# GRU gates of a recurrent block on one core: r and z share 64-row passes, their sigmoids run in halves, and VectorE copies the turned h

## The reference

```
adj  = relu(x.reshape(b, 1600) @ masker_param[t] + masker_bias[t]), rows normalised   # b, t, 50, 50
m    = adj @ (x @ weight)                                                             # b, t, 50, 32
gates = m @ w_ih.T + b_ih + x @ w_hh.T + b_hh ; r, z, ng = split(gates, 3)
r = sigmoid(r); z = sigmoid(z); ng = tanh(r * ng)
h = (1 - z) * ng + z * x
... batch norm over the 2048 samples, layer norm per sample, attention over the nodes, weighted sum -> (b, 64)
```

## Time and profile before

| | |
|---|---|
| time of three runs, median (lowest to highest) | 2565.87 us (2556.56 to 2578.45) |
| the profiled execution's own time | 2563.58 us |
| its span | 2561.6 us |
| mean granted TensorE clock | 0.965 of full speed |
| TensorE matmul, busy | 2367.9 us, 92% |
| TensorE weight load, busy | 1913.5 us, 75% |
| VectorE, busy | 1049.4 us, 41% |
| ScalarE, busy | 814.4 us, 32% |
| GpSimd, busy | 560.3 us, 22% |

### The profile page before, as it was taken

How to read it: one execution, slowest core, us unless ns; L and a number is a source line. 1 busy time by engine, 2 the same in 40 slices (tenths; PEclk the granted TensorE clock), 3 DMA queues, 4 the chain that set the end, 5 groups by cost and what they waited for, 6 DMA issues and landing times. The chain is left out here.

```text
span 2561.6 us, 34873 instructions
## 1 busy us (share of the span) xinstructions
PE 2367.9 (92%) x12466; PEld 1913.5 (75%) x12466; DVE 1049.4 (41%) x1771; ACT 814.4 (32%) x1353; POOL 560.3 (22%) x365
## 2 busy tenths in 40 slices
PE   6899999999979999999999994999999999975788
PEld 4788888888867888888888873888888888852333
DVE  3432233333224333223333312565656666575446
ACT  2321222222223222122222212444444444535341
POOL 0000000000000000000000000567677676764130
PEclk9999999999999999999999996999999999987889
DMA  5412222221244211222222005454545455318430
GB/s 152 121 67 83 83 83 83 83 80 43 70 133 134 82 51 62 83 83 83 83 83 81 30 28 164 132 166 131 170 134 158 142 154 153 118 63 236 122 88 5
DMA packets 178886, 262.63 MB, mean 103 GB/s; under 512 B 11370, under 2 KB 160558, under 8 KB 175534
## 3 DMA queue, kind: packets, MB, share of 16 engines
q1 hardware_dynamic: 162706, 235.74, 30.6%
q10 hardware_dynamic: 16128, 26.22, 2.9%
HBM read 194.22 MB, written 67.70 MB: 102 GB/s over the span
## 5 line engine op out<-in xcount | busy, mean ns | idle before, releaser
L326 PE MATMUL psum<-w_hi,x_lo 128*128 128x500 f32 x2080 | 826.6, 397 | 32.2 <-DVE x_lo L187 15.6
L326 PE MATMUL psum<-w_lo,x_hi 128*128 128x500 f32 (+1 forms) x2080 | 814.4, 392 | 0.0
L326 PE MATMUL psum<-w_hi,x_hi 128*128 128x500 f32 x1920 | 749.7, 390 | 0.0
L326 PEld LDWEIGHTS psum<-w_hi,x_lo 128*128 128x128 f32 x2080 | 394.1, 189 | 111.2 <-issue 20.6
L267 DVE TENSOR_REDUCE rows<-u 128x10 f32<-128x500 f32 x160 | 107.6, 672 | 895.4 <-ACT u L221 895.0
L326 PEld LDWEIGHTS psum<-w_lo,x_hi 128*128 128x128 f32 (+1 forms) x2080 | 395.1, 190 | 75.7
L326 PEld LDWEIGHTS psum<-w_hi,x_hi 128*128 128x128 f32 x1920 | 363.6, 189 | 74.3
L620 POOL MEMSET share<- 128x1 f32 x1 | 0.1, 98 | 1540.0 <-POOLq L79 1540.0
L227 ACT COPY at<-psum 128x640 f32<-128x640 f32 x160 | 110.7, 692 | 690.6 <-PE psum L308 690.6
L686 PE MATMUL psum<-adj_sb,xs_sb 100*64 100x100 f32 x2048 | 200.6, 350 | 30.5 <-DMA xs_sb<-xz 30.5
L686 PEld LDWEIGHTS psum<-adj_sb,xs_sb 100*64 100x64 f32 x2048 | 145.0, 149 | 73.4 <-issue 63.7
(11 more groups left out here) (169 smaller groups left out, 2832.6 us busy)
## 6 DMA issues: line engine op xcount, KB each, us to landing
w_raw<-W SPq DMA_DIRECT2D x120, 500.0 KB, 6.7
adjT<-at SPq DMA_DIRECT2D x320, 125.0 KB
adj_sb<-adjT SPq DMA_DIRECT2D x16, 2500.0 KB
xs_sb<-xz SPq DMA_DIRECT2D x16, 1600.0 KB
hF<-hC ACTq DMA_DIRECT2D x96, 256.0 KB, 3.5
h<-hF SPq DMA_DIRECT2D x64, 256.0 KB, 4.2
x_raw<-xT SPq DMA_DIRECT2D x16, 832.0 KB
xg_sb<-xg SPq DMA_DIRECT2D x16, 800.0 KB, 19.6
```

Of the source, the lines that this page charges most:

```text
L326: last = nc.tensor.matmul(mm_out(w % 2), a[0:r, k, cols], b[0:r, k, :], start=k == 0 and n == 0, stop=k == KF and n == 1)
```

## The change

- r and z no longer have passes of their own. The weights `wd` hold two sets of 128 columns: `RZ_W`, in which the rows of two sample groups (64 rows) lead to 128 outputs, r and z of both, and `N_W`, block-diagonal as before. For each of the six terms two matmuls are issued, one on rows 0 to 63 into bank 2, one on rows 64 to 127 into bank 3. In bank 2 r of its two groups is in partitions 0 to 63 and z in 64 to 127, in bank 3 the other way round, so that r lies where n of the same group lies, and z is in the other half.
- n comes after the turns now, and `gates_done` after n. The r-z block waits for `r_ready` and `z_ready` of the round before.
- Each sigmoid is two instructions of 64 partitions. z's write to a fourth bank (`z_bank`, bank 4, one for all rounds) in the other partition half and wait for `h_ready` of the round before.
- VectorE makes the copy of the turned chunks (`evacuate`), between `update` and `finish`, and after the last tile all seven batches ahead of its statistics. ScalarE issues the store after z's sigmoids and before the tanh.
- The setup on VectorE copies the weights in 24 pieces instead of 8.

```diff
-        wd = sb("wd", [P, 2, 3, P])
+        wd = sb("wd", [P, 2, 2, P])
-        gate_done = [sem(f"{g}_done") for g in ("r", "z", "n")]
+        rz_done, gates_done = sem("rz_done"), sem("gates_done")
+        def rz_bank(pair):
+            return psum[:, (2 + pair) * BANK:(2 + pair) * BANK + RC]
+        z_bank = psum[:, 4 * BANK:4 * BANK + RC]
+        n_bank = lambda s: psum[:, (5 + s % 2) * BANK:(5 + s % 2) * BANK + RC]
...
 ScalarE, in turn():
-                    if q and (r or not (isinstance(it, int) and it == 0)):
-                        evacuate(it * 2 + r - 1, q - 1)
                     if s + 1 < S or more:
-                        wait(act, gate_done[Z_G], it * S + s)
+                        wait(act, gates_done, it * S + s)
                         m_halves(it + (s + 1) // S, (s + 1) % S)
-                    if q and (r or not (isinstance(it, int) and it == 0)):
-                        store(it * 2 + r - 1, q - 1)
                     k = s % ROUNDS - (ROUNDS - 1 - XPARTS)
                     if 0 <= k < XPARTS and (s < ROUNDS or more):
                         x_hi(it + s // ROUNDS, 1 - s // ROUNDS, k)
-                    act.wait_ge(gate_done[R_G], it * S + s + 1)
+                    act.wait_ge(rz_done, it * S + s + 1)
                     wait(act, n_in_ready, it * S + s)
-                    nc.scalar.activation(r_gate[:], gate_bank(R_G, s), ACT.Sigmoid,
-                                         bias=bias[:, R_G:R_G + 1]).then_inc(r_ready, 1)
-                    act.wait_ge(gate_done[Z_G], it * S + s + 1)
-                    nc.scalar.activation(gate_bank(Z_G, s), gate_bank(Z_G, s), ACT.Sigmoid,
-                                         bias=bias[:, Z_G:Z_G + 1]).then_inc(z_ready, 1)
+                    for pair in range(2):
+                        half = slice(SH * pair, SH * pair + SH)
+                        last = nc.scalar.activation(r_gate[half], rz_bank(pair)[half], ACT.Sigmoid, bias=bias[half, R_G:R_G + 1])
+                    last.then_inc(r_ready, 1)
+                    wait(act, h_ready, it * S + s)
+                    for pair in range(2):
+                        half, other = slice(SH * pair, SH * pair + SH), slice(SH - SH * pair, 2 * SH - SH * pair)
+                        last = nc.scalar.activation(z_bank[half], rz_bank(pair)[other], ACT.Sigmoid, bias=bias[other, Z_G:Z_G + 1])
+                    last.then_inc(z_ready, 1)
+                    if q and (r or not (isinstance(it, int) and it == 0)):
+                        store(it * 2 + r - 1, q - 1)
                     act.wait_ge(n_in_ready, it * S + s + 1)
-                    nc.scalar.activation(gate_bank(N_G, s), n_in[:, s % 2], ACT.Tanh).then_inc(n_ready, 1)
+                    nc.scalar.activation(n_bank(s), n_in[:, s % 2], ACT.Tanh).then_inc(n_ready, 1)
...
 VectorE:
+            def evacuate(tile, n):
+                dve.wait_ge(turned, tile * len(batches) + n + 1)
+                wait(dve, hC_stored[n], 16 * tile)
+                c0, c1 = batches[n]
+                nc.vector.tensor_copy(hC[:, c0:c1, :].rearrange("p c b -> p (c b)"),
+                                      turn_bank[:, 0:(c1 - c0) * P]).then_inc(hC_ready, 1)
...
                     update(it, s)
+                    if s % ROUNDS and (s > ROUNDS or not (isinstance(it, int) and it == 0)):
+                        evacuate(it * 2 + s // ROUNDS - 1, s % ROUNDS - 1)
...
             for k in range(1, TPARTS):
                 turn_rows(TILES // 2 - 1, 1, k)
+            for n in range(len(batches)):
+                evacuate(TILES - 1, n)
...
 TensorE, in gates():
+                wait(pe, r_ready, it * S + s)
+                wait(pe, z_ready, it * S + s)
+                for w, m, first, final in terms(RZ_W):
+                    for pair in range(2):
+                        half = slice(SH * pair, SH * pair + SH)
+                        last = nc.tensor.matmul(rz_bank(pair), w[half], m[half], start=first, stop=final)
+                last.then_inc(rz_done, 1)
+                if q and (r or not (isinstance(it, int) and it == 0)):
+                    turn_chunks(it * 2 + r - 1, q - 1)
+                wait(pe, h_ready, it * S + s - 1)
+                for w, m, first, final in terms(N_W):
+                    last = nc.tensor.matmul(n_bank(s), w, m, start=first, stop=final)
+                last.then_inc(gates_done, 1)
```

More of the change, by code:

```diff
@@ L61 @@
 R_G, Z_G, N_G = 0, 1, 2
+RZ_W, N_W = 0, 1
 FQ = P // D
@@ L390, in stage2 @@
         bias = sb("bias", [P, 3])
-        wd = sb("wd", [P, 2, 3, P])
-        wd_hi = sb("wd_hi", [P, 2, 3, P], fp32r)
-        wd_lo = sb("wd_lo", [P, 2, 3, P], fp32r)
+        wd = sb("wd", [P, 2, 2, P])
+        wd_hi = sb("wd_hi", [P, 2, 2, P], fp32r)
+        wd_lo = sb("wd_lo", [P, 2, 2, P], fp32r)
         means, devs = stats
@@ L466, in x_hi @@
                     act.wait_ge(xg_loaded[r], (it + 1) * 16)
-                    wait(act, gate_done[Z_G], it * S if r else it * S - ROUNDS)
+                    wait(act, gates_done, it * S if r else it * S - ROUNDS)
                 g = slice(k * XG, (k + 1) * XG)
@@ L474, in m_halves @@
                 nc.scalar.copy(m_hi[:, s % 2], ax_bank(s)).then_inc(m_hi_ready, 1)
[L476 to L482, removed]
             def store(tile, n):
@@ L520, in _ @@
             for n in range(len(batches)):
-                evacuate(TILES - 1, n)
                 store(TILES - 1, n)
@@ L531, in _ @@
                 q = slice(D * j, D * j + D)
-                nc.vector.tensor_copy(wd[q, 0, :, q], psum[q, 0:3 * D].rearrange("p (g e) -> p g e", g=3))
-                last = nc.vector.tensor_copy(wd[q, 1, :, q], whh4[q, :].rearrange("p (g e) -> p g e", g=3))
+                pair, one = divmod(j, 2)
+                at = {R_G: SH * pair + D * one, Z_G: SH - SH * pair + D * one, N_G: D * j}
+                for gate, first in at.items():
+                    of, e = (N_W if gate == N_G else RZ_W), slice(D * gate, D * gate + D)
+                    nc.vector.tensor_copy(wd[q, 0, of, first:first + D], psum[q, e])
+                    last = nc.vector.tensor_copy(wd[q, 1, of, first:first + D], whh4[q, e])
             last.then_inc(blocks_ready, 1)
@@ L549, in update @@
             def update(it, s):
-                dve.wait_ge(gate_done[N_G], it * S + s + 1)
+                dve.wait_ge(gates_done, it * S + s + 1)
                 dve.wait_ge(r_ready, it * S + s + 1)
-                nc.vector.scalar_tensor_tensor(out=n_in[:, s % 2], in0=gate_bank(N_G, s), scalar=bias[:, N_G:N_G + 1],
+                nc.vector.scalar_tensor_tensor(out=n_in[:, s % 2], in0=n_bank(s), scalar=bias[:, N_G:N_G + 1],
                                                in1=r_gate[:], op0=ALU.add, op1=ALU.mult).then_inc(n_in_ready, 1)
@@ L560, in finish @@
                 dve.wait_ge(n_ready, it * S + s + 1)
-                diff, n_gate, z_gate = n_in[:, s % 2], gate_bank(N_G, s), gate_bank(Z_G, s)
+                diff, n_gate = n_in[:, s % 2], n_bank(s)
                 x_b = xg[:, r, q].unsqueeze(1).to_broadcast([P, T, N * QB])
@@ L699, in gates, with terms @@
                 xb = [t[:, r, q].unsqueeze(1).to_broadcast([P, T, N * QB]) for t in (xg_hi, xg_lo)]
-                for gate in (R_G, N_G, Z_G):
-                    if gate == Z_G:
-                        if q and (r or not (isinstance(it, int) and it == 0)):
-                            turn_chunks(it * 2 + r - 1, q - 1)
-                        wait(pe, h_ready, it * S + s - 1)
-                    elif gate == N_G:
-                        wait(pe, h_ready, it * S + s - 1)
-                    else:
-                        wait(pe, r_ready, it * S + s)
-                    terms = []
-                    for part, (hi, lo) in enumerate(((m_hi[:, s % 2], m_lo[:, s % 2]), xb)):
-                        terms += [(wd_lo[:, part, gate], hi), (wd_hi[:, part, gate], lo), (wd_hi[:, part, gate], hi)]
-                    for i, (w, m) in enumerate(terms):
-                        last = nc.tensor.matmul(gate_bank(gate, s), w, m, start=i == 0, stop=i == len(terms) - 1)
-                    last.then_inc(gate_done[gate], 1)
+                def terms(of):
+                    found = []
+                    for part, (hi, lo) in enumerate(((m_hi[:, s % 2], m_lo[:, s % 2]), xb)):
+                        found += [(wd_lo[:, part, of], hi), (wd_hi[:, part, of], lo), (wd_hi[:, part, of], hi)]
+                    return [(w, m, i == 0, i == 5) for i, (w, m) in enumerate(found)]
+                wait(pe, r_ready, it * S + s)
[11 more added lines that the diff above has]
+                last.then_inc(gates_done, 1)
             def turn_chunks(tile, n):
```

5 lines of the change are left out of this document (1 added, 4 removed).

## The result

| | before | after |
|---|---|---|
| median of four runs each, side by side | 2561.22 us (2554.99 to 2578.45) | 2591.93 us (2586.87 to 2596.84) |
| ratio, 95% interval | | 1.0092 [1.0065, 1.0118] |
| profiled execution, its span | 2563.58, 2561.6 us | 2596.84, 2595.0 us |
| mean granted TensorE clock | 0.965 | 0.937 |

The kernel became 0.9% slower: 24 us by the ratio. In the later runs, made for the experiments, the kernel before had medians of 2568.1 to 2569.0 us (7 to 23 runs), which is 23 to 24 under 2591.93, so the ratio is the better measure than the difference of these two medians. It stands just inside the line of 1% that the prediction drew between "same" and "slower" (by the two medians alone it would be 1.2%); 2585 was forecast.

The account below looks back on a forecast made before the run. The bound was taken to be the tile's loop of adj issue, xg's landing and two rounds, not TensorE. Beginning -4, tiles +13, end -1, tail +10 gave +18 to +19; 2563.6 + 19 + 2.3 = 2585 us, range 2544 to 2615.

Parts of the forecast that it names:

- The loop: Each tile: adj issue, DMA, xg landing, cast, sigmoids, two TensorE rounds, next adj issue; 44.1 us without the clock.
- A to L: From SyncE's issue of a later tile's adj load to the landing of xg: 31.9 to 32.0 us, unmoved.
- The pair: Two 64-row r and z matmuls on TensorE: 0.22 us, bounds 0.18 and 0.36; a round 4.64 against 5.40.
- L to A: From the landing of xg to the next adj issue: 12.1 us against 12.2, without the lower clock.
- The serial sigmoids: Round 3, four halves of 0.49 us behind the cast of xg: landing to round 4 takes 2.55 against 1.15.
- The clock: TensorE stands some 4 us before round 4, lower clock in most tiles: 1.3 us a tile, bounds 0.3 and 2.5.
- Beginning: Tile 0, six rounds to the first adj issue, 5.04 before and 4.28 after: -4 us, bounds 0 and -5.
- End: From the last landing of xg to the last h: 64.2 plus 1.3 for the clock, against 66.2 us: -1.
- The tail: After the last tile, VectorE's seven copies delay its statistics; the stage ends 10 us later, bounds 8 and 12.
- B: TensorE's clock stays up, tile 44.4 us as before: +5, 2571 us; chance 0.18.
- C: TensorE's row halves don't overlap: block 2.16, tile 45.8 plus 0.8 of clock, 2608 us; chance 0.17.
- D: xg lands under 30 us after adj's issue; GpSimd's loop through xg_lo gives 42.2 us a tile: 2542 us; chance 0.15.

Follow-up runs that it names:

- Experiment 3: The changed kernel with all six r and z matmuls of bank 2 issued before the six of bank 3: 2610.01 us, 1.0153 of the kernel before.
- experiment 5: The changed kernel with SyncE issuing xg ahead of xs on the same queue: 2546.58 us, 0.9907 of the kernel before.
- experiment 1: The changed kernel with xg loaded on ScalarE's queue instead of SyncE's: 2576.94 us, 1.0018 of the kernel before.
- experiment 4: The changed kernel with 36 extra unread matmuls in round 4 before the wait for r_ready: 2565.29 us, 0.9997 of the kernel before.
- experiment 8: The changed kernel with the seven copies after the last tile back on ScalarE: 2583.43 us, 1.0056 of the kernel before.
- experiment 7: The changed kernel, load order as changed, with the cast of xg moved behind the tanh: 2548.37 us, 0.9917 of the kernel before.

## Why the prediction was right, and where its sizes were off

It said 2585, +19, with 0.57 on "within 1%"; measured are +0.9% and 24.7 us in the parts that the change touches. The mechanism was the forecast one. Term by term:

- **The loop.** A to L was to stay at 32, and nearly did: 32.3 over 14 (30.7 to 34.2), and 32.5 over the 13 that make up the tiles, where the kernel before had 31.8. These 0.5 a tile over the 32.0 of the sum are 6 of the us that it missed; whether the change causes them isn't shown. Experiment 3 shows it from one side (61 us more matmul work cost 16), experiment 5 from the other (the wait gone, the time falls). What experiment 1 took away is the explanation by the order of one queue: behind the stores of another queue, which take turns with adj and xs, xg is as late.
- **The pair** was taken at 0.22 and is 0.18, the lower bound. The round is 4.47 instead of 4.64. In the two rounds from L to A this is 0.3 less than forecast; in the six others it only lengthens the wait.
- **The serial sigmoids**: 2.78 from L to round 4 instead of 2.55, since a half takes 0.55 from start to start and not 0.49, like a whole one. They cost 1.6 us a tile against before, and the two shorter rounds give back 1.9. Without the clock L to A would be 12.0, the 12.1 of the prediction; experiment 4 has 12.0 to 12.4.
- **The clock** is the term that was mis-sized. "It stands some 4 us at once" became 6.7 to 10.0 (4.9 in the first tile), because the tile is longer, VectorE's chain is 38.5 and not 40.0 (each of its rounds 0.15 to 0.26 shorter), and TensorE's rounds are 0.17 shorter. Every tile now loses the upper level, where 1.3 us was put on the mean. Losing it costs 6.89 - 4.47 = 2.4 us in the tile shown and 14.1 - 12.0 = 2.1 on the mean: 14.1 from L to A instead of 13.4, or 9 us over 13 tiles. With the 6 of A to L that makes +28.6 over the 13 tiles instead of +13. That the idleness is the cause is shown by experiment 4.
- **Beginning** -3.8 (forecast -4); this piece took 59.6 to 64.1 us in profiles of kernels that share the changed beginning, so the close fit is in part luck. **End** -6.3 (forecast -1): the last xg landed 30.7 after its A (2213.53 to 2244.27), 1.4 sooner than before, and from there to the last h are 61.2 us (forecast 64.2 and 1.3 for the clock): the rounds there are paced by VectorE, whose chain was priced too long.
- **The tail** +6.2 (forecast +10). The copies take what was forecast (from 2309.17, one each 1.96 us), and the statistics start at 2320.45, 14.9 behind the last h. But VectorE then works alone, GpSimd being through at 2319.2: 8.9 us for what takes 12.4 in the earlier trace rows, where VectorE also stands behind instructions of GpSimd, as the rows of experiment 8 show. The squares take 4.16 there and 2.16 alone (the kernel after).
- **Rivals.** B (2571, the clock stays up) is what experiment 4 builds, and it comes to 2565. C (2608) is refuted by pairs 0.18 apart. D (2542) didn't happen for want of an early xg; experiment 5 made xg early, experiment 7 took its landing out of the loop, and both found D's loop at 43.0 to 43.6 instead of 42.2, at 2547 and 2548 us. The remainder is the lower clock in round 0, which the sum left out.

The terms of the sum were off by +16, -5 and -4, which partly cancel: by luck 2585 is nearer to 2592 than its working was.

What stays open: the clock fell in the changed kernel after each of the 14 waits of 4.9 to 10.0 us, and in the one before after 3.00 but not after 2.48. In the trace of the kernel before it also fell after 1.55 (first matmul at 1641.01, clock 0.50 in the window 1641 to 1644) and not after 2.40 (2086.16, 1.00 in 2086 to 2090), so the length of the wait alone doesn't decide; what does isn't settled here.

## What to carry to other kernels

Look for the loop that paces a tile (the distance from one issue of a load to the next, cut at the landing) before pricing an engine's work: an engine at 96% can still be inside a loop that another sets, and what it saves outside the piece from landing to next issue becomes idleness. Long idleness of TensorE has its own price through the clock, here 2.1 us a tile on the mean, so a saving that isn't passed on can cost. When one bound is removed, price the next two. Here the landing of xg and then GpSimd's xg_lo hid a change worth 2.5%, and VectorE's wait behind a store, which the change itself had made, held another 38 us. Moving loads and instructions took 6.2% off the changed kernel, more than its shorter matmul blocks were worth.

## What the runs showed of the hardware

- Two fp32r matmuls of 64 rows and 400 columns on different row halves take 0.18 us a pair, as one of 128 rows does, both weight loads included. The Trainium skill ("TensorE: Matmul & The Clock Gate", Part 3) says that distinct row groups run together, and the trace agrees; by the load time that its Part 2 gives, 107 ns for 128 columns whatever the rows, an estimate for two loads one after the other is 0.214, more than the pair takes. So either the loads overlap as well, or one takes under 0.09; these rows don't tell which.
- Issued bank by bank (experiment 3) the second half's first matmul starts 0.47 behind the first half's first, before the first half's fourth (1797.77): the two streams overlapped, and the block lost 0.47, not the 0.9 of twelve in a row. The Trainium skill's same page (Part 2) says that matmuls stay in program order; the recorded starts of this trace differ.
- A queue of its own did not bring the landing of xg (0.8 MB) nearer to A. In the changed kernel it was 21.0 us from issue to landing on the median, against 21.1 on the shared queue. In the kernel before it was 17.2 against 19.6, and yet A to L stayed (31.6 against 31.9).
- A sigmoid on 64 partitions takes as long as on 128: r's 590 ns on the mean of 256, against 0.59 us.
- VectorE beside GpSimd: 4.16 against 2.16 us for 1920 squares a partition, 1.68 against 0.19 for a TENSOR_SCALAR of 60 elements, and GpSimd's squares 4.34 against 2.32. In the rows of experiment 8 each of the three ends as if it had started when the other engine's instruction ended: they ran one after the other, and did not share. The reductions took 2.11 to 2.15 in both cases.
